# Two cross-attention layers on one core: ScalarE's read of the first V bank moves behind the exps of score tile 3

## The chip, the core and the metric

The kernel runs on one core of a Trainium2 chip. The core has five engines with a queue of instructions each, which run in program order and meet only through semaphores: TensorE (matrix products into the PSUM banks), VectorE, ScalarE (exp and scaled copies), GpSimd and SyncE (here it only starts DMAs). The metric is the device time of one execution in microseconds (us).

## The reference, cut to what matters

Two layers of cross-attention with 20 heads of 32 columns, 8 batches of 100 queries and a context of 722 tokens: 77 text tokens and 645 more tokens ("ip"), which have weights of their own. Each layer takes the softmax over text and over ip apart and adds the two results. Layer 1 also adds a term to the ip scores, computed from the text attention, and multiplies the ip probabilities by a mask.

```python
k, v = heads(text @ Wk), heads(text @ Wv)
k_ip, v_ip = heads(ip @ Wk_ip), heads(ip @ Wv_ip)
text_out = softmax(q @ k.T * scale) @ v
fused = q @ k_ip.T * scale + (0.5 * sem if layer == 1 else 0)   # sem: [b, q, ip token]
ip_out = softmax(fused) * (mask if layer == 1 else 1) @ v_ip
x = (text_out + ip_out) @ Wout + bias + x
```

## The kernel before, in words

The products of context and weights are made from pairs of 16-bit numbers: each operand is split into a high and a low part, and three matmuls (high x high, high x low, low x high) stand for one. So every K or V bank is read twice when it is done: ScalarE writes the high part as a scaled copy (k_unit L1083, v_unit L1091), and VectorE writes the low part as bank minus high part (L1625, L1635). VectorE's instruction waits for ScalarE's (v_high), and its own end sets v_low or k_low, which frees the bank.

A layer has 40 steps u: 8 batches i times 5 groups g of 4 heads. In step u, TensorE does the following in an order written out by hand (window, L808): the V product of step n = u + 1 (five tiles of 24 matmuls, v_tile, three in bank A of `proj`, two in bank B), the six score tiles of step u (score_tile, L695, into the two banks `st`), the weighing of V with the probabilities (weigh, L718), the K product of step k = u + 2 (k_part, in banks A and B again) and the row maxima of the scores of step n (max_scores, L675 and L676). Bank A is therefore used in each step first for V of step n and then for K of step k, and the first k_part of bank A waits for v_low of bank A (L645). Where there is no step k, rows of the output product stand in its place (out_tile).

ScalarE's order in a step (L1133): for each of the six score tiles two exps, one for the high part in 16 bits (L1107) and one in 32 bits (L1108). The end of both is p_high. Score tile j + 2 goes to the same bank and waits for it, and so do the low parts of the probabilities, made by VectorE (tiles 0, 2, 4, L1670) and GpSimd (tiles 1, 3, 5, L1347). Between the tiles stand the reads of the two V banks, in layer 0 slices of the next context (split_context, L1020, groups 1 and 2), and the copy of the transposed output (o_turn, L1114), which frees the buffer `rows` for its next use. In layer 1 VectorE adds the semantic term to each score tile first (add_semantic, L1751), and ScalarE's exps wait for that addition. VectorE's order has its part of the first V bank (L1635) behind prob_low of tile 2 and ahead of add_semantic of tiles 4 and 5.

Some steps of layer 1 hold more (for the first seven batches): group 2 the text logits, group 3 the 48 matmuls of text_ip between weigh 2 and k_part, group 4 turn_semantic (L772), six transposes between v_tile 5 and weigh 1, which write `rows` when o_turn's copy has freed it.

Of the kernel before, what the change touches and what calls it, by code (L numbers as in the profile page):

```python
# [71 lines left out]
def xattn_pair_kernel(nc, ctx_d, text_d, x_d, w_d, wq_d, wo_d, bias_d, mask_d, const_d, sel_d, kd, qd, vd, cd, out_d):  # L72
    with ExitStack() as stack:
# [135 lines left out]
        def need(eng, s, n):  # L209

            if n > 0:
                eng.wait_ge(s, n)
# [17 lines left out]
        def sums(u):  # L230

            return NT * (u - STEPS)

        def low_done(eng, u, j):

            if j < 0:
                u, j = u - 1, j + NT
            if u >= 0:
                mine = [t for t in range(NT) if on_pool(t) == on_pool(j)]
                eng.wait_ge(p_low[on_pool(j)], u * len(mine) + mine.index(j) + 1)  # L240
# [35 lines left out]
        for l in range(LAYERS):  # L276
# [5 lines left out]
            for i in range(B):  # L282
                for g in range(G):
                    u = l * STEPS + i * G + g
# [27 lines left out]
        def placed(n, each):  # L312

            return each * (n // 2 + 1)

        def scales(r):

            return rs[:, r % 2] if r < B else rs1[:, r - B]
# [5 lines left out]
        def scaled(eng, r):  # L324

            eng.wait_ge(row_scale, min(r, B) + 1)
# [9 lines left out]
        def exists(u, l):  # L336

            return u < (l + 1) * STEPS
# [643 lines left out]
        def _(act):  # L982
# [33 lines left out]
            def split_context(r, k):  # L1016

                if k % 2:
                    act.wait_ge(ctx_scaled, r * (KT // 2) + (k // 2 + 1))
                nc.scalar.activation(c_part(r % 2, 0)[:, k, :], ctx_raw[:, k, :], ACT.Copy,  # L1020
                                     scale=1.0 if k % 2 else csb[:, r, 0:1]).then_inc(ctx_high, 1)
# [11 lines left out]
            def q_split(r):  # L1033

                act.wait_ge(q_chain, 5 * (r // B) + 5)
                need(act, qw_out, 16 * r)
                if r > B:
                    row_done(act, "logit", r - B - 1)
                nc.scalar.activation(qhl[:, 0, 0:G * S].rearrange("p (g q) -> p g q", g=G), q_rows(r),
                                     ACT.Copy, scale=qs[:, 4:5]).then_inc(q_hi_ok, 1)  # L1040
# [36 lines left out]
            def k_unit(n, c):  # L1077

                act.wait_ge(k_full, 2 * n + (c + 1))
                if c == 0:  # L1080
                    need(act, kw_out[0], 16 * n)
                a, w = (0, N0) if c == 0 else (N0, N1)
                nc.scalar.activation(khl[:, 0, a:a + w], banks[c][:, 0:w], ACT.Copy, scale=VSC).then_inc(k_high, 1)  # L1083

            def v_unit(n, c):

                act.wait_ge(v_full, 2 * n + (c + 1))
                if c == 0:
                    need(act, pv_tile, NT * (n - 1))
                a, b, src = (2, 2 + VA, bankA) if c == 0 else (2 + VA, NT + 1, bankB)  # L1090
                nc.scalar.activation(vst[:, n % 2, a:b, :, D:2 * D].rearrange("p t h d -> p (t h) d"),  # L1091
                                     src[:, 0:(b - a) * P].rearrange("p (n d) -> p n d", d=D), ACT.Copy,
                                     scale=VSC).then_inc(v_high, 1)

            def exps(u, j):

                r = u // G
                if u >= STEPS:
                    act.wait_ge(s_sum, sums(u) + j + 1)
                else:  # L1100
                    act.wait_ge(s_full, u * NT + (j + 1))
                low_done(act, u, j - 3)
                need(act, pv_tile, (u - 1) * NT + j + 1)
                if j == 0:
                    scaled(act, r)
                scale = scales(r)[:, 4:5] if j == 0 else scales(r)[:, 1:2]
                nc.scalar.activation(p_hi[:, j, 0:Q4], st[:, j % 2, 0:Q4], ACT.Exp, scale=scale)  # L1107
                nc.scalar.activation(prob[:, j % 3, :], st[:, j % 2, 0:Q4], ACT.Exp, scale=scale).then_inc(p_high, 1)  # L1108

            def o_turn(u):  # L1110

                row_filled(act, "oT", u)
                i, g = u // G % B, u % G
                nc.scalar.activation(qo[:, g, i * S:(i + 1) * S], rows[:, 0, 0:S], ACT.Copy).then_inc(row_free, 1)  # L1114

            def logits(i):

                r = B + i
                row_filled(act, "logit", i)
                act.wait_ge(probs, i * 5 + 2)  # L1120
                nc.scalar.activation(pr[:, 0:TEXT], rows[0:S, 0, 0:TEXT], ACT.Exp, bias=sm[:, 1:2],
                                     scale=scales(r)[0:S, 0:1]).then_inc(row_free, 1)

            def turn_semantic(i):

                row_filled(act, "semT", i)
                if i >= 2:
                    act.wait_ge(s_sum, sums((B + i - 1) * G))
                nc.scalar.activation(sem_t[:, i % 2, 1:].rearrange("p n q -> p (n q)"), rows[:, 0, 0:(NT - 1) * S],
                                     ACT.Copy)  # L1130
                nc.scalar.activation(sem_t[:, i % 2, 0], rows[:, 1, 0:S], ACT.Copy).then_inc(row_free, 1)

            def window(l, i, g):  # L1133

                u, r = l * STEPS + i * G + g, l * B + i
                n, k = u + 1, u + 2
                more, more2 = exists(n, l), exists(k, l)
                splits = iter(SLICES[4 * (g - 1):4 * g] if l == 0 and i < B - 1 and g in (1, 2) else ())

                def split():  # L1140
                    for k in splits:
                        split_context(r + 1, k)
                        break

                if u % STEPS and more:
                    k_unit(n, 1)
                exps(u, 0)
                if l == 0 and i < B - 1 and g == 1:
                    act.wait_ge(ctx_chain, 5 * (r + 1) + 5)
                    if r >= 1:  # L1150
                        act.wait_ge(c_out[(r + 1) % 2], placed(r - 1, 32))
                    else:
                        act.wait_ge(w_low, 16)
                split()
                exps(u, 1)
                if l and i < B - 1 and g == 2:
                    logits(i + 1)
                split()
                exps(u, 2)
                if more:  # L1160
                    v_unit(n, 0)
                exps(u, 3)
                if u % STEPS:
                    o_turn(u - 1)
                split()
                if l and i < B - 1 and g == 4:
                    turn_semantic(i + 1)
                exps(u, 4)
                if more:
                    v_unit(n, 1)  # L1170
                exps(u, 5)
                split()
                if g == 1 and i < B - 1:
                    q_split(r + 1)
                if more2:
                    k_unit(k, 0)
# [51 lines left out]
            for i in range(B):  # L1228
                for g in range(G):
                    if i == B - 1 and g == G - 1:  # L1230
                        load_weight(1, 0), load_weight(1, 1)
                    window(0, i, g)
# [36 lines left out]
            for i in range(B):  # L1269
                for g in range(G):  # L1270
                    window(1, i, g)
# [789 lines left out]
```

## Time and profile before

| | us |
|---|---|
| median of 3 runs | 1762.08 (1761.41 to 1764.46) |
| the profiled execution, its own time | 1764.17 |
| its span in the trace | 1762.0 |
| TensorE busy | 1742.4 (99%) |
| VectorE busy | 1197.9 (68%) |
| ScalarE busy | 777.5 (44%) |
| GpSimd busy | 426.0 (24%) |

The granted clock of TensorE was full over the whole span. The score tiles run from 137.9 to 1736.9 us of the span, in two loops, one for each layer; in front of each stand the projections and the splitting of the weights. "PE" is a matmul, "PEld" the load of its weights, which can run beside the matmuls ahead of it. A time in brackets behind a row is what the engine idled before it, with the one it waited for.

### The profile page before, as it was taken

Reading aid. Unit: us, or ns where it says so; the run is one execution under the profiler, and the core shown is the slowest. Engines: PE = TensorE matmul, PEld = TensorE weight load, DVE = VectorE, ACT = ScalarE, POOL = GpSimd, SP = SyncE. Lnnn points to the kernel's source line nnn. Section 1 sums busy time; section 2 is a strip of 40 time slices with the busy share of each in tenths; the row PEclk is TensorE's granted clock in tenths of the full one; section 3 lists DMA queues with packets and bytes.
Section 4 is the critical chain, followed back from the end, with each engine's and each line's share of the span. In section 5 each row is a group of like instructions: output and inputs, shape, how many; then the busy total and the mean of one; then the engine's idle time right before and its main releaser. Section 6 shows DMA issues by size and latency. Waiting matters only on the chain.

```text
span 1762.0 us, 51994 instructions
## 1 busy us (share of the span) xinstructions
PE 1742.4 (99%) x22067; PEld 1413.0 (80%) x22067; DVE 1197.9 (68%) x2905; ACT 777.5 (44%) x1569; POOL 426.0 (24%) x523
## 2 busy tenths in 40 slices
PE   8999999999999999999999999999999999999999
PEld 4778888888888888886577888888888888888885
DVE  6877676767676767554745567767676767676674
ACT  3334555455555555543322344534353435344342
POOL 3034342433333333311100112211121212122111
PEclk9999999999999999999999999999999999999999
DMA  8652535343434343444146232423141323233221
GB/s 324 125 163 105 164 112 156 113 134 113 133 115 131 120 126 123 123 126 179 60 82 177 68 94 81 109 75 101 45 138 45 121 69 109 60 99 92 82 66 47
DMA packets 124015, 198.37 MB, mean 113 GB/s; under 512 B 41752, under 2 KB 110760, under 8 KB 116936
## 3 DMA queue, kind: packets, MB, share of 16 engines
q1 hardware_dynamic: 118600, 168.44, 33.1%
q10 hardware_dynamic: 5184, 26.60, 4.0%
q8 instruction: 175, 2.87, 0.7%
q14 instruction: 56, 0.46, 0.1%
HBM read 133.91 MB, written 60.88 MB: 111 GB/s over the span
## 4 chain that ended last, share of the span: by engine, by line
PE 93%; DVE 3%; DMA 2%; ACT 1%; issue 0%; SPq 0%; POOL 0%; ACTq 0%
PE proj L562 65%; PE proj L522 7%; PE pv L718 6%; PE st L695 5%; PE rows L675 4%; PE rows L562 3%; PE rows L676 2%; DMA arena<-k_dram 1%; DMA k_dram<-arena 1%; DVE wparts L1435 1%; PE rows L763 1%; DMA extra<-x_dram 0%; PE rows L726 0%; PE proj L627 0%; DVE t_hl L1478 0%
## 5 line engine op out<-in xcount | busy, mean ns | idle before, releaser
L562 PE MATMUL proj<-w_hl,cbuf 128*128 128x128 f16 x9600 | 601.0, 219 | 1.2 <-ACT odd_both L1072 1.2
L562 PE MATMUL proj<-cbuf,w_hl 128*128 128x322 f16 (+1 forms) x3840 | 591.5, 300 | 0.3 <-DVE arena L1625 0.3
L562 PEld LDWEIGHTS proj<-w_hl,cbuf 128*128 128x128 f16 x9600 | 548.4, 98 | 3.8 <-ACT odd_both L1072 1.9
L562 PEld LDWEIGHTS proj<-cbuf,w_hl 128*128 128x128 f16 x3840 | 367.7, 97 | 163.5 <-DVE arena L1625 0.6
L1347 POOL TENSOR_TENSOR arena<-arena 128x400 f16<-128x400 f32 x240 | 233.8, 974 | 866.8 <-ACT arena L1108 866.7
L1107 ACT ACTIVATE arena<-st,rs 128x400 f16<-128x400 f32 x480 | 287.3, 598 | 268.3 <-DVE st L1751 158.4
L1083 ACT ACTIVATE arena<-proj 128x323 f16<-128x323 f32 (+1 forms) x160 | 70.7, 442 | 490.2 <-PE proj L562 490.2
L1108 ACT ACTIVATE arena<-st,rs 128x400 f32<-128x400 f32 x480 | 285.7, 595 | 0.0
L1670 DVE TENSOR_TENSOR arena<-arena 128x400 f16<-128x400 f32 x240 | 141.8, 591 | 118.2 <-ACT arena L1108 114.6
L718 PEld LDWEIGHTS pv<-arena 128*128 128x128 f16 x3840 | 175.5, 97 | 25.0 <-issue 4.3
L1751 DVE TENSOR_TENSOR st<-st,sem_t 128x400 f32<-128x400 f32 x240 | 135.3, 579 | 87.1 <-PE st L695 85.3
L718 PE MATMUL pv<-arena 128*128 128x34 f16 (+3 forms) x3840 | 192.4, 189 | 0.0
L1642 DVE TENSOR_REDUCE mx<-rows 100x1 f32<-100x77 f32 x320 | 75.7, 236 | 126.4 <-PE rows L676 126.2
L695 PE MATMUL st<-arena 128*128 128x100 f16 x1920 | 151.5, 207 | 2.2 <-DVE arena L1665 1.4
L1646 DVE CUSTOM_DVE_ANT_0 raw<-rows,raw 100x645 bf16<-100x645 f32 x160 | 131.8, 824 | 0.0
L1650 DVE TENSOR_REDUCE mx<-rows 100x1 f32<-100x645 f32 x160 | 131.1, 819 | 0.0
L675 PE MATMUL rows<-arena 96*128 96x512 f16 x320 | 121.3, 379 | 3.5 <-DMA arena<-k_dram 1.8
L695 PEld LDWEIGHTS st<-arena 128*128 128x128 f16 x1920 | 108.8, 97 | 6.9 <-ACT arena L1108 2.2
L1625 DVE SCALAR_TENSOR_TENSOR arena<-proj,arena 128x323 f16<-128x323 f32 (+1 forms) x160 | 79.0, 494 | 49.2 <-ACT arena L1083 46.4
L676 PE MATMUL rows<-arena 96*128 96x229 f16 x320 | 84.0, 262 | 0.0
L1635 DVE SCALAR_TENSOR_TENSOR arena<-proj,arena 128x384 f16<-128x384 f32 (+1 forms) x160 | 77.3, 483 | 2.0 <-ACT arena L1091 2.0
L1091 ACT ACTIVATE arena<-proj 128x384 f16<-128x384 f32 (+1 forms) x160 | 70.8, 442 | 13.4 <-PE proj L562 13.4
(169 smaller groups left out, 1624.9 us busy)
## 6 DMA issues: line engine op xcount, KB each, us to landing
arena<-k_dram SPq DMA_DIRECT2D x240, 185.2 KB, 3.6
k_dram<-arena SPq DMA_DIRECT2D x160, 161.2 KB, 1.9
raw<-ctx_dram SPq DMA_DIRECT2D x16, 1290.0 KB, 7.7
c_dram<-cbuf SPq DMA_DIRECT2D x16, 1290.0 KB, 6.4
cbuf<-c_dram SPq DMA_DIRECT2D x14, 1290.0 KB, 6.3
cbuf<-w_dram ACTq DMA_DIRECT2D x24, 640.0 KB, 8.0
arena<-q_dram SPq DMA_DIRECT2D x48, 125.0 KB, 2.6
w_hl<-w_dram ACTq DMA_DIRECT2D x8, 640.0 KB, 11.5
```

The lines of the kernel that those rows point to most:

```text
L522: mm = nc.tensor.matmul(bank[:, 0:MT], weight[:, c, k], src[:, k], start=(k == 0), stop=(k == CT - 1))
L562: mm = nc.tensor.matmul(out, x[a](k), w[b](k), start=(k == 0 and m == 0), stop=(k == KT - 1 and m == 2))
L675: nc.tensor.matmul(rows[:, 0, :], q, kp[0:IPO, n % 2, h, 0:512], start=True, stop=True)
L695: mm = nc.tensor.matmul(st[:, j % 2, h * S:(h + 1) * S], kp[:, u % 2, h, a:b], qp[:, r % 2, q_col(g, h):q_col(g, h) + S], start=True, stop ...
L718: mm = nc.tensor.matmul(out, p[:, j, h * S:h * S + P], v, start=(j == 0 and h % 2 == 0 and m == 0), stop=(j == NT - 1 and h % 2 == 1 and m ...
L1107: nc.scalar.activation(p_hi[:, j, 0:Q4], st[:, j % 2, 0:Q4], ACT.Exp, scale=scale)
L1108: nc.scalar.activation(prob[:, j % 3, :], st[:, j % 2, 0:Q4], ACT.Exp, scale=scale).then_inc(p_high, 1)
L1347: nc.gpsimd.tensor_tensor(p_lo[:, j, 0:Q4], prob[:, j % 3, :], p_hi[:, j, 0:Q4], ALU.subtract).then_inc(p_low[1], 1)
L1646: last = nc.vector.tensor_tensor_reduce(out=junk, in0=rows_f[0:S, IPO:KW], in1=semq[r % 2], scale=1.0, scalar=LOWEST, op0=ALU.add, op1=ALU ...
L1650: last = nc.vector.tensor_reduce(mx[:, 1, h:h + 1], rows_f[0:S, IPO:KW], AX.X, ALU.max)
L1670: nc.vector.tensor_tensor(p_lo[:, j, 0:Q4], prob[:, j % 3, :], p_hi[:, j, 0:Q4], ALU.subtract).then_inc(p_low[0], 1)
L1751: nc.vector.tensor_tensor(tile, tile, term, ALU.add).then_inc(s_sum, 1)
```

## The change

In ScalarE's order of each step, the read of the first V bank (v_unit(n, 0)) stands behind the two exps of score tile 3 in place of ahead of them. It concerns the 78 steps that have a next one in their layer. No other engine's order changes.

```diff
@@ -1157,9 +1157,9 @@
                     logits(i + 1)
                 split()
                 exps(u, 2)
+                exps(u, 3)
                 if more:
                     v_unit(n, 0)
-                exps(u, 3)
                 if u % STEPS:
                     o_turn(u - 1)
                 split()
```

ScalarE in an ordinary step of layer 1, before; the first two rows are the exps of tile 2, `proj` is the V bank (the first bank is the one read as 12x32, the second 8x32), `st` a score tile, `rows` the transposed output:

```order
L1107 ACTIVATE arena<-st,rs 128x400 [waits pv_tile,p_low_pool,s_sum]
L1108 ACTIVATE arena<-st,rs 128x400
L1091 ACTIVATE arena<-proj 128x12x32 [waits pv_tile,v_full]
L1107 ACTIVATE arena<-st,rs 128x400 [waits pv_tile,p_low_dve,s_sum]
L1108 ACTIVATE arena<-st,rs 128x400
L1114 ACTIVATE qo<-rows 128x100 [waits row_full]
L1107 ACTIVATE arena<-st,rs 128x400 [waits pv_tile,p_low_pool,s_sum]
```

The same place now:

```order
L1107 ACTIVATE arena<-st,rs 128x400 [waits pv_tile,p_low_pool,s_sum]
L1108 ACTIVATE arena<-st,rs 128x400
L1107 ACTIVATE arena<-st,rs 128x400 [waits pv_tile,p_low_dve,s_sum]
L1108 ACTIVATE arena<-st,rs 128x400
L1091 ACTIVATE arena<-proj 128x12x32 [waits pv_tile,v_full]
L1114 ACTIVATE qo<-rows 128x100 [waits row_full]
L1107 ACTIVATE arena<-st,rs 128x400 [waits pv_tile,p_low_pool,s_sum]
```

The read has gone from the place ahead of the exps of tile 3, which wait for the addition on the tile (s_sum), to the place ahead of the copy of the transposed output.

ScalarE in a step of layer 0 with group 1, before and now; L1020 is a slice of the next context:

```order
L1020 ACTIVATE cbuf<-raw,csb 128x645
L1107 ACTIVATE arena<-st,rs 128x400 [waits pv_tile,p_low_pool,s_full]
L1108 ACTIVATE arena<-st,rs 128x400
L1091 ACTIVATE arena<-proj 128x12x32 [waits pv_tile,v_full]
L1107 ACTIVATE arena<-st,rs 128x400 [waits pv_tile,p_low_dve,s_full]
L1108 ACTIVATE arena<-st,rs 128x400
L1114 ACTIVATE qo<-rows 128x100 [waits row_full]
L1020 ACTIVATE cbuf<-raw 128x645 [waits ctx_scaled]
```

```order
L1020 ACTIVATE cbuf<-raw,csb 128x645
L1107 ACTIVATE arena<-st,rs 128x400 [waits pv_tile,p_low_pool,s_full]
L1108 ACTIVATE arena<-st,rs 128x400
L1107 ACTIVATE arena<-st,rs 128x400 [waits pv_tile,p_low_dve,s_full]
L1108 ACTIVATE arena<-st,rs 128x400
L1091 ACTIVATE arena<-proj 128x12x32 [waits pv_tile,v_full]
L1114 ACTIVATE qo<-rows 128x100 [waits row_full]
L1020 ACTIVATE cbuf<-raw 128x645 [waits ctx_scaled]
```

Here the exps wait for the score tile itself (s_full), and the read passes the same two rows.

## Rows read from the trace of the kernel before

**Rows 1.** The page's chain of work that ended last: share of the span by engine.
```profile
PE 93%; DVE 3%; DMA 2%; ACT 1%; issue 0%; SPq 0%; POOL 0%; ACTq 0%
```

**Rows 2.** Two stretches: length, busy us of each engine, clock, DMA share, GB/s.
```profile
150.00:800.00 650.00, 646.84 (x9271) 547.75 (x9267) 454.47 (x1082) 335.38 (x692) 223.37 (x248) 1.00 0.40 125
...
1000.00:1700.00 700.00, 697.99 (x9681) 586.08 (x9679) 488.83 (x1315) 305.79 (x649) 138.16 (x190) 1.00 0.31 89
```

**Rows 3.** Timeline, ordinary step of layer 1: start us, us, engine, line, operation.
```profile
1200.90 0.34 PE L695 MATMUL st<-arena 128*128 128x100 f16 x4
...
1201.28 0.58 DVE L1751 TENSOR_TENSOR st<-st,sem_t 128x400 f32<-128x400 f32 x1 [0.93 <-PE st L695]
...
1201.35 0.49 ACT L1091 ACTIVATE arena<-proj 128x384 f16<-128x384 f32 x1
...
1201.90 0.59 ACT L1107 ACTIVATE arena<-st,rs 128x400 f16<-128x400 f32 x1
...
1202.25 0.55 DVE L1635 SCALAR_TENSOR_TENSOR arena<-proj,arena 128x384 f16<-128x384 f32 x1
...
1202.87 0.25 ACT L1114 ACTIVATE qo<-rows 128x100 f32<-128x100 f32 x1
...
1203.48 1.06 DVE L1751 TENSOR_TENSOR st<-st,sem_t 128x400 f32<-128x400 f32 x2 [0.68 <-PE st L695]
...
1203.66 0.67 PEld L562 LDWEIGHTS proj<-cbuf,w_hl 128*128 128x128 f16 x6
...
1203.68 0.99 PE L562 MATMUL proj<-cbuf,w_hl 128*128 128x323 f16 x6
```

**Rows 4.** Timeline, first V bank of layer 1, both readers waiting.
```profile
980.31 0.49 ACT L1091 ACTIVATE arena<-proj 128x384 f16<-128x384 f32 x1 [2.21 <-PE proj L562]
...
980.83 0.56 DVE L1635 SCALAR_TENSOR_TENSOR arena<-proj,arena 128x384 f16<-128x384 f32 x1 [0.88 <-ACT arena L1091]
```

**Rows 5.** Timeline, ordinary step of layer 0.
```profile
459.89 0.34 PE L695 MATMUL st<-arena 128*128 128x100 f16 x4
...
460.27 0.59 ACT L1107 ACTIVATE arena<-st,rs 128x400 f16<-128x400 f32 x1
...
461.24 0.25 ACT L1114 ACTIVATE qo<-rows 128x100 f32<-128x100 f32 x1
...
462.64 0.67 PEld L562 LDWEIGHTS proj<-cbuf,w_hl 128*128 128x128 f16 x6
```

**Rows 6.** Timeline, a step of layer 0 with group 1.
```profile
425.68 0.50 ACT L1091 ACTIVATE arena<-proj 128x384 f16<-128x384 f32 x1
...
426.05 0.61 ACT L1107 ACTIVATE arena<-st,rs 128x400 f16<-128x400 f32 x1
...
426.53 0.62 ACT L1108 ACTIVATE arena<-st,rs 128x400 f32<-128x400 f32 x1
...
427.20 0.20 PEld L695 LDWEIGHTS st<-arena 128*128 128x128 f16 x4 [0.19 <-ACT arena L1108]
...
427.60 1.09 PEld L562 LDWEIGHTS proj<-cbuf,w_hl 128*128 128x128 f16 x9
```

**Rows 7.** Timeline, a step of layer 1 with group 4.
```profile
1261.86 0.49 ACT L1091 ACTIVATE arena<-proj 128x384 f16<-128x384 f32 x1
...
1263.74 0.46 PEld L772 LDWEIGHTS rows<-const,raw 100*128 100x128 f32 x5 [0.37 <-issue]
...
1265.09 0.67 PEld L562 LDWEIGHTS proj<-cbuf,w_hl 128*128 128x128 f16 x6
```

**Rows 8.** Who waited for whom: us in total, times, longest us.
```profile
PEld rows L683 <- DVE mxh L1658: 15.4, 77, 0.8
...
PE rows L772 <- ACT qo L1114: 1.6, 7, 0.2
...
PE rows L683 <- DVE mxh L1658: 0.6, 1, 0.6
```

## The prediction, made before the changed kernel had run

> **What bounds the kernel now.** I read the page's chain first, then the stretches of the two layers, the waits of TensorE and of its weight loads, and at last single steps of the timeline. In the chain the reader is to see that TensorE holds 93% of the time [rows 1]. In the long loop of layer 0 it leaves 650.00 - 646.84 = 3.2 us open, in that of layer 1 700.00 - 697.99 = 2.0 us [rows 2]. So the most that any reordering of ScalarE can win in both loops is 5.2 us, 0.3% of the time, while each new wait of TensorE lands on the end in full. The question is what TensorE next asks of bank A of the product `proj`: k_part of the step after next overwrites it and waits for v_low, which VectorE sets when it has read the bank, and VectorE subtracts what ScalarE wrote, so it waits for ScalarE's read.
>
> **The change.** It removes and adds no instruction. In each of the 78 steps that have a next one in their layer ScalarE's read of the first V bank goes behind the two exps of score tile 3. On ScalarE it passes only those two; ScalarE's DMAs stand outside the steps and keep their places. Queued behind the read in its new place: the copy of the transposed output (L1114), a context slice, the exps of tile 4. Queued behind VectorE's part of that bank (L1635): in layer 1 the additions for tiles 4 and 5, in layer 0 a context slice or row maxima.
>
> Do the exps start sooner? In an ordinary step of layer 1 the read runs 1201.35 to 1201.84; the addition on tile 3 ends 1201.28 + 0.58 = 1201.86, and the exps start at 1201.90 [rows 3]. They wait for that addition, 0.04 behind it, and the read lay wholly inside this wait. In an ordinary step of layer 0 score tile 3 ends 459.89 + 0.34 = 460.23 and the exps start at 460.27 [rows 5]. So in both the exps of tile 3 can't start sooner, ScalarE loses a free place for its read, and the read is pushed behind 0.97 us of exps (1201.90 to L1114's start at 1202.87 [rows 3]).
>
> Layer 1, ordinary step [rows 3]: read of V at 1202.87, end + 0.49 = 1203.36. VectorE takes over 0.03 behind such an end: 980.31 + 0.49 = 980.80, start 980.83 [rows 4]. So L1635 runs 1203.39 to 1203.94 (0.55 each). TensorE follows a VectorE or ScalarE end 0.05 later (426.53 + 0.62 = 427.15, load at 427.20 [rows 6]), so its first weight load of k_part is possible at 1203.99 and now stands at 1203.66 [rows 3]: a wait of 0.33, say 0.34 us. Before, L1635 ended at 1202.80 and there were 0.86 us to spare. All links of the chain hang on TensorE's own score tile 3, so a later start in the step before does not pay any of it back: each step pays.
>
> How many steps? Groups 0, 1 and 2 of eight batches, 24. In group 3 of the first seven, the 48 long matmuls of text_ip stand ahead of k_part, in group 4 the turn of the semantic term pushes k_part to 1265.09 - 1261.86 = 3.23 us behind the old read, against 2.31 in the ordinary step [rows 7, 3]; both cover 0.34. In the last batch group 3 has no k_part. 24 x 0.34 = **8.2 us**.
>
> Group 4 of the first seven batches pays elsewhere. The copy L1114 now stands behind the moved read: it starts one spacing of that read later, 426.05 - 425.68 = 0.37 us [rows 6]. TensorE's turn of the semantic term waits for this copy today (0.37 us idle ahead of its weight load [rows 7], 1.6 us of matmul time in seven cases [rows 8]). 7 x 0.37 = **2.6 us**. In the other groups the next user of that row buffer comes behind weigh 2, when the copy (new end 1203.24 + 0.25 = 1203.49) is done.
>
> VectorE's additions for tiles 4 and 5 follow L1635: 1203.48 becomes about 1203.86, so the exps of tile 4 and the second V read come 0.38 us later. What waits for these are weigh 4 and k_part on bank B, several matmul groups behind; I cost it at nothing, and if that cover were gone it would be 0.38 per step more.
>
> Layer 0, ordinary step [rows 5]: read 461.24 to 461.73, L1635 461.76 to 462.31, load possible at 462.36, wanted at 462.64: 0.28 us to spare, no wait. In groups 0 and 4 VectorE has context maxima in front of L1635 anyway.
>
> Layer 0, group 1 of seven batches: here ScalarE lags, since it splits the context, and the exps of tile 3 really start sooner, at 425.68 where the read stood, in place of 426.05. The wait of 0.19 us in front of score tile 5 goes [rows 6], 7 x 0.19 = 1.3 us and no more. But bank A: read 426.64 (two spacings of 0.48 behind 425.68), end 427.14, L1635 427.17 to 427.72, load possible at 427.77, today 427.60. What comes late next is this: the gained 0.19 turns into a wait in front of k_part and 0.17 beyond it. 7 x 0.17 = **1.2 us**.
>
> Sum: 8.2 + 2.6 + 1.2 = 12.0 us. Against the profiled execution (1764.2 us, span 1762.0) that is 1776.2; it stood 2.1 us above the median of the runs, 1762.1, and on this median I forecast **1774.1 us**.
>
> Bounds. From below: TensorE's loads run ahead of its matmuls, so a load that waits is not always a matmul that waits. The transpose of the maxima shows it: 77 waits of its load are 15.4 us, but its matmul is listed with 0.6 us, once [rows 8]. There the matmul in front is a long one. In front of k_part stand the short ones of weigh 2, and load and matmul of k_part begin 0.02 apart (1203.66 and 1203.68 [rows 3]), so I take the load's wait as the matmul's. Would each wait be softened by 0.15, the sum is 24 x 0.19 + 7 x 0.22 + 7 x 0.02 = 6.2 us. The Trainium skill ("TensorE: Matmul & The Clock Gate", on what happens when a matmul is issued) says that the queue pulls weight loads ahead of running matmuls while the matmuls keep their order; by that rule the softening is there wherever a long matmul runs in front, and for the transpose the trace agrees (15.4 us of loads, 0.6 us of matmuls).
> From above: if the exps and the read did not overlap at their ends (0.59 + 0.59 in place of 0.97), every chain is 0.21 longer: 24 x 0.55 + 7 x 0.37 + 7 x 0.38 = 18.5 us.
> The Trainium skill ("ScalarE: Activation LUTs", What ACT_TABLE_LOAD costs) gives an activation 186 ns plus 0.833 per element, 93 more for a scale by pointer and 93 less back to back. As an estimate that spaces the exps by 0.52 us, where the trace has 0.49; by the page the sum would be some 2 us larger, and the trace decides.
>
> **Rivals.**
> *Half price*: the softening above. For it: the transpose [rows 8]. Against: the 0.02 between load and matmul. +6 us, 1768.
> *Covered*: VectorE's read fits, because the moved read finds a gap or k_part starts later than I read. For it: in layer 0 the spare place exists. Against: every ordinary step of layer 1 repeats those times [rows 3]. Only the seven copies remain, 2.6 us, 1764.7, or nothing.
> *Knock-on*: the 0.38 us on the exps of tiles 4 and 5 reaches weigh 4, or layer 0's 0.28 us is used up by slower reads. 24 x 0.38 = 9 us more, 1783. Against: weigh 4 stands two groups of k_part matmuls behind.
> *Faster*: score tile 5 and GpSimd's low part of tile 3 wait for the exps of tile 3, so these set the step wherever ScalarE lags, and the read can wait. It is decided by whether ScalarE is late at tile 3: only the seven steps of layer 0 show that. It would win at most 7 x 0.19 plus one longer first wait, some 1.7 us, 1760.4, and beyond the 5.2 us of open time nothing. It needs that bank A is never late, against [rows 3, 6].
>
> **How the numbers follow.** Full price (1770 to 1778) 0.74; half price 0.10; knock-on or the upper bound 0.07; covered 0.06; faster 0.03. A measurement of this kernel can tell 0.2%, 3.5 us, from no change. Half price and all above it are slower: 0.91. Covered gives within 0.2%; faster, as worked out, stays mostly within it too, and I leave 0.02 for more. The range leaves out the knock-on and the covered case: 1768 to 1779.
>
> **What would show it.** Right: the read of V about 1.5 us later in an ordinary step; in layer 1 a wait of proj's loads for L1635 on the list, about 24 to 31 times and 8 to 10 us; L772 waiting for L1114 with some 0.6 us each; exps of tile 3 as far behind score tile 3 as before; the steps of layer 0 outside group 1 as long as before. Wrong: no such wait in layer 1; ordinary steps of layer 0 longer; a wait of weigh 4 for L1670, or exps of tile 3 that start sooner in layer 1.

## The result: 14.1 us slower, 8 of them in 24 steps of layer 1

The changed kernel takes 1775.87 us (median of 6 runs, 1775.27 to 1777.75), the kernel before 1761.74 us (6 runs, 1761.09 to 1764.46): 14.1 us more, ratio 1.0079 [1.0066, 1.0092]. The forecast was 1774.1 us in a range of 1768 to 1779.

The profiled execution took 1775.68 us (span 1773.5). The page's chain, shares of the span by engine:

```profile
PE 86%; DVE 5%; ACT 4%; issue 2%; POOL 1%; DMA 1%; SPq 0%; ACTq 0%
```

TensorE had 93% of the chain [rows 1]; VectorE and ScalarE now have 9% in place of 4%. The stretches of both layers, columns as in [rows 2]:

```profile
150.00:800.00 650.00, 646.91 (x9266) 547.04 (x9263) 455.35 (x1080) 335.41 (x693) 225.91 (x248) 1.00 0.40 125
1000.00:1700.00 700.00, 691.77 (x9529) 578.54 (x9528) 481.98 (x1295) 301.21 (x641) 136.19 (x187) 1.00 0.31 88
```

In layer 1 TensorE's open time grew from 2.0 to 700.00 - 691.77 = 8.2 us. In layer 0 it did not grow (3.1 us), and yet some of its steps got longer, as shown below: the stretch of before holds 1.6 us in which matmuls waited for K loads, that of the changed kernel none, and this hides the new waits. The waits that answer to [rows 8], and the new ones:

```profile
PEld rows L683 <- DVE mxh L1658: 15.0, 77, 0.8
PEld proj L562 <- DVE arena L1635: 9.3, 31, 0.4
PE proj L562 <- DVE arena L1635: 6.0, 31, 0.3
...
PEld rows L772 <- issue: 5.2, 7, 0.7
...
PE rows L772 <- ACT qo L1114: 4.2, 7, 0.6
...
PEld pv L718 <- POOL arena L1347: 2.7, 7, 0.4
...
PE rows L683 <- DVE mxh L1658: 0.6, 1, 0.6
```

The first two new ones were forecast: k_part waits 31 times for VectorE's part of bank A, and L772 waits longer for the copy L1114. The wait of the weighing (L718) for GpSimd's low part was not. The step that answers to [rows 3], timeline:

```profile
1205.22 0.58 DVE L1751 TENSOR_TENSOR st<-st,sem_t 128x400 f32<-128x400 f32 x1 [0.94 <-PE st L695]
...
1205.83 0.59 ACT L1107 ACTIVATE arena<-st,rs 128x400 f16<-128x400 f32 x1 [0.44 <-DVE st L1751]
...
1206.80 0.49 ACT L1091 ACTIVATE arena<-proj 128x384 f16<-128x384 f32 x1
...
1207.17 0.26 ACT L1114 ACTIVATE qo<-rows 128x100 f32<-128x100 f32 x1
...
1207.32 0.56 DVE L1635 SCALAR_TENSOR_TENSOR arena<-proj,arena 128x384 f16<-128x384 f32 x1 [1.05 <-ACT arena L1091]
...
1207.80 1.05 DVE L1751 TENSOR_TENSOR st<-st,sem_t 128x400 f32<-128x400 f32 x2
1207.93 0.66 PEld L562 LDWEIGHTS proj<-cbuf,w_hl 128*128 128x128 f16 x6 [0.28 <-DVE arena L1635]
1207.94 1.00 PE L562 MATMUL proj<-cbuf,w_hl 128*128 128x323 f16 x6 [0.17 <-DVE arena L1635]
```

The exps of tile 3 start 1205.83 - (1205.22 + 0.58) = 0.03 us behind the addition, as before: nothing was won. ScalarE now idles 0.44 us ahead of them, where it had read V. The read comes 0.97 behind the start of the exps, VectorE's part 0.52 behind the read, k_part's load 0.61 behind that.

To see what a wait costs, the steps are measured: from TensorE's transpose of the maxima (L683), which ends each step, to the next one, less the same step of the kernel before. In us per step, changed kernel:

| layer | groups | steps | longer by |
|---|---|---|---|
| 0 | 0, 3, 4, the last batch | the others | 0 |
| 0 | 1, first seven batches | 7 | -0.02 to 0 |
| 0 | 2, first seven batches | 7 | 0.41 |
| 1 | 0, 1, 2 | 24 | 0.33 to 0.35 (22 of them) |
| 1 | 3, first seven batches | 7 | 0 |
| 1 | 4 | 7 | 0.38 |
| 1 | 3 of the last batch, the last step with a next one | 1 | 0.30 |

24 x 0.34 + 7 x 0.38 + 7 x 0.41 + 0.30 = 14.0 us. The other steps are within 0.03, except single ones, mostly those in which, in one of the two executions, TensorE waits for a DMA of K (1.8 us of such matmul waits in the profiled execution of before, none listed in the changed kernel's; the first step of layer 1's batch 3 is 0.05 shorter here and 1.2 longer in e11). Such waits come and go from kernel to kernel, and by them the spans of the two profiled executions differ by only 11.5 us. So costs are read here from repeated steps, and the medians only with their intervals.

### The profile page after: what moved, and what is told of

The parts are those of the page before. It is cut to its first block, busy times and chain, and to the rows that moved or that the text cites. A ratio compares the mean times of both kernels' runs of the same rounds, so it can differ in the third digit from the quotient of the medians.

```text
span 1773.5 us, 51994 instructions
## 1 busy us (share of the span) xinstructions
PE 1745.6 (98%) x22067; PEld 1413.2 (80%) x22067; DVE 1199.7 (68%) x2905; ACT 776.7 (44%) x1569; POOL 428.3 (24%) x523
## 4 chain that ended last, share of the span: by engine, by line
PE 86%; DVE 5%; ACT 4%; issue 2%; POOL 1%; DMA 1%; SPq 0%; ACTq 0%
PE proj L562 61%; PE proj L522 6%; PE pv L718 5%; PE rows L675 4%; PE st L695 4%; PE rows L562 3%; ACT arena L1108 2%; PE rows L676 2%; DVE arena L1635 1%; DMA mask<-mask_dram 1%; DVE st L1751 1%; ACT arena L1091 1%; POOL arena L1347 1%; DVE wparts L1435 1%; PE rows L763 1%
## 5 line engine op out<-in xcount | busy, mean ns | idle before, releaser
L1347 POOL TENSOR_TENSOR arena<-arena 128x400 f16<-128x400 f32 x240 | 234.0, 975 | 875.0 <-ACT arena L1108 874.9
L1670 DVE TENSOR_TENSOR arena<-arena 128x400 f16<-128x400 f32 x240 | 145.7, 607 | 97.8 <-ACT arena L1108 94.6
L718 PEld LDWEIGHTS pv<-arena 128*128 128x128 f16 x3840 | 174.8, 97 | 27.1 <-issue 4.3
L718 PE MATMUL pv<-arena 128*128 128x34 f16 (+3 forms) x3840 | 192.5, 189 | 0.3
L1650 DVE TENSOR_REDUCE mx<-rows 100x1 f32<-100x645 f32 x160 | 131.0, 818 | 0.0
L675 PE MATMUL rows<-arena 96*128 96x512 f16 x320 | 121.3, 379 | 1.5 <-DVE mx L1650 0.5
L1635 DVE SCALAR_TENSOR_TENSOR arena<-proj,arena 128x384 f16<-128x384 f32 (+1 forms) x160 | 77.8, 486 | 60.8 <-ACT arena L1091 60.8
```

The source lines that it names most:

```text
L675: nc.tensor.matmul(rows[:, 0, :], q, kp[0:IPO, n % 2, h, 0:512], start=True, stop=True)
L718: mm = nc.tensor.matmul(out, p[:, j, h * S:h * S + P], v, start=(j == 0 and h % 2 == 0 and m == 0), stop=(j == NT - 1 and h % 2 == 1 and m ...
L1347: nc.gpsimd.tensor_tensor(p_lo[:, j, 0:Q4], prob[:, j % 3, :], p_hi[:, j, 0:Q4], ALU.subtract).then_inc(p_low[1], 1)
L1650: last = nc.vector.tensor_reduce(mx[:, 1, h:h + 1], rows_f[0:S, IPO:KW], AX.X, ALU.max)
L1670: nc.vector.tensor_tensor(p_lo[:, j, 0:Q4], prob[:, j % 3, :], p_hi[:, j, 0:Q4], ALU.subtract).then_inc(p_low[0], 1)
```

## Experiments

The first four runs compare parts of the change, against a kernel before of 1764.22 us. Each `late` is the condition under which the read stands in its new place.

**e1, the change in layer 0 alone**, and **e2, in layer 1 alone**:

```diff
                 exps(u, 2)
-                if more:
+                late = l == 0        # e2: l == 1
+                if more and not late:
                     v_unit(n, 0)
                 exps(u, 3)
+                if more and late:
+                    v_unit(n, 0)
```

> The read of the first V bank behind the exps of tile 3 in layer 0 alone; layer 1 as before. Theory A (the cost of layer 0 sits in group 2 of the first seven batches, where GpSimd's context slice and the low part of tile 3 queued behind it come late): +0.41 us in each of those seven steps, nothing in the other groups, +2.9 us in all. Theory B (my prediction: a wait for bank A in group 1): seven times 0.17, +1.2 us. Theory C (the difference between the two traces in layer 0 is only chance in the waits for k_dram loads): within 1 us, and no step longer by a fixed amount.

> The read behind the exps of tile 3 in layer 1 alone. Theory A (TensorE waits for bank A 24 times by 0.34 us, for the copy L1114 seven times by 0.37, and once by 0.3 in front of the output product of the last step): +11.1 us, the layer 1 steps exactly as long as with the whole change, so that both layers add up to the whole. Rival (the two layers act on each other over the weights and the turn between them): less or more than the rest that layer 0 leaves of 14.1 us.

e1: 1767.84 us against 1764.22, ratio 1.0015 [1.0004, 1.0025]. Steps: group 2 +0.40 to 0.41, seven times, group 1 nothing, layer 1 nothing. e2: 1774.13, ratio 1.0053 [1.0036, 1.0071]; layer 0 nothing, layer 1 as in the changed kernel (0.34, 0.38 and 0.34 for the last). The steps of the two halves add up to those of the whole, so neither cost depends on the other layer's change.

**e3, layer 1 alone, and in group 4 the copy ahead of the moved read:**

```diff
+                if late and g == 4 and u % STEPS:
+                    o_turn(u - 1)
                 if more and late:
                     v_unit(n, 0)
-                if u % STEPS:
+                if u % STEPS and not (late and g == 4):
                     o_turn(u - 1)
```

> As the change in layer 1 alone, but in group 4 the copy of the transposed output (L1114) stands ahead of the moved read. Theory A: the seven group 4 steps lose nothing any more (0.37 less each, 2.6 us less than the change in layer 1 alone), since k_part has over 0.5 us to spare there for a read 0.25 us later; +8.5 us. Rival (group 4 is long because the exps of tiles 4 and 5 are late): those steps stay 0.37 longer, +11.1 us.

Group 4's steps fall from +0.38 to 0 (within 0.01), the ordinary ones stay at 0.34. The waits of L772:

```profile
PEld rows L772 <- issue: 2.6, 7, 0.4
PE rows L772 <- ACT qo L1114: 1.6, 7, 0.2
```

So group 4 pays for the copy and for nothing else. The time itself was not lower than e2's: 1776.14 us, ratio 1.0058 [1.0035, 1.0081], 6.2 to 14.3 us. In the profiled execution the stretch between the two loops, in which the projections of layer 1 stand and which the edit doesn't touch, is 4.2 us longer. The interval holds the 8.5 us of the steps, and e2's time too: only the steps tell e3 from e2.

**e4, only where the steps say it is free** (layer 0 without group 2 of the first seven batches, and layer 1, group 3 of the same):

```diff
+                late = (l == 0 and (g != 2 or i == B - 1)) or (l == 1 and g == 3 and i < B - 1)
```

> The change only in steps where it should cost nothing: layer 0 except group 2 of the first seven batches, layer 1 only group 3 of the first seven. 32 + 7 = 39 steps have the new order. Theory A: no step differs by more than 0.03 us, time within 0.5 us of before. Prediction's theory B for group 1: +1.2 us. Rival (the new order costs a little everywhere, as ScalarE idles ahead of the exps and then works longer): 39 steps x 0.1 or more, +4 us.

1765.03 us against 1764.22, ratio 1.0003 [0.9993, 1.0013]. The steps with group 1 are within 0.02 although their k_part waits (2.6 us of its loads in seven cases). Nothing is gained in them either.

The next four runs ask what a wait of k_part costs, and what happens in group 2. The time of the kernel before is 1762.07 us beside them.

**e6, the read behind the copy too**, in all steps:

```diff
                 exps(u, 3)
-                if more:
-                    v_unit(n, 0)
                 if u % STEPS:
                     o_turn(u - 1)
+                if more:
+                    v_unit(n, 0)
```

> The dose: the read behind the exps of tile 3 and behind the copy L1114 (0.25 us more, by the spacing of L1114 to what follows). Theory A (the chain score tile 3, addition, exps, read, VectorE's part, k_part sets the step in layer 1): 24 ordinary steps wait 0.34 + 0.21 to 0.25 = 0.55 to 0.59, group 4 waits nothing for the copy, layer 0 ordinary steps have 0.28 to spare and lose 0 to 0.03, group 1 and 2 lose up to 0.25 and 0.4: 13.7 + 0.5 + 2.9 to 4.6 = +17 to +19 us. Rival (the additions of tiles 4 and 5 are what is late): the same order of VectorE, so about the same; it differs in the next run.

1779.21 us, ratio 1.0093 [1.0076, 1.0110]. Ordinary steps of layer 1 +0.48 to 0.49, group 4 nothing, group 2 of layer 0 +0.54 to 0.55, group 1 +0.04 to 0.06. The read ends 0.15 later than in the changed kernel, where 0.21 to 0.25 was expected, since it begins while the copy still runs. The step is 0.15 longer: 0.15 of lateness buys 0.15 of length, with no softening.

**e7, the first two maxima matmuls ahead of the first k_part**, layer 1, groups 0 to 2, on the changed kernel:

```diff
+                first = l == 1 and g < 3
+                if first:
+                    max_scores(n, 0)
                 if more2:
                     k_part(k, 0, 0, begun)
-                max_scores(n, 0)
+                if not first:
+                    max_scores(n, 0)
```

> The whole change, and TensorE does the first row maxima of the next step (2 matmuls, 0.32 us by their spacing) ahead of the first k_part in groups 0, 1, 2 of layer 1, where they stood behind six of its matmuls. Theory A: TensorE has work while bank A is read, the 24 waits of 0.34 fall to 0.02, 7.7 us less than the whole change, so +6.4 us. Rival (the layer 1 cost comes from the additions for tiles 4 and 5 and the exps behind them, which stay as late as in the whole change): +14.1 us, no less. If the maxima have a wait of their own so early (k_dram loads, the row buffer), some of it comes back under another name.

The ordinary steps fall from +0.34 to +0.02 or 0.03: with other work in front of k_part, the lateness of bank A costs next to nothing. VectorE's additions for tiles 4 and 5 still come late here, so these cost nothing either. Its loads are still listed with a long wait, its matmuls no longer outside layer 0 (there 1.8 us, as in the changed kernel):

```profile
PEld proj L562 <- DVE arena L1639: 7.9, 30, 0.5
...
PE proj L562 <- DVE arena L1639: 1.8, 7, 0.3
```

(L1639 is L1635 with four lines more in front.) The time: 1772.37 us, ratio 1.0056 [1.0041, 1.0071], 7.2 to 12.5 us above before. The steps give 24 x 0.02 + 0.1 + 2.7 + 2.9 + 0.3 = 6.5. The rest of the run's difference stays open; the profiled execution has 1.8 us of K waits, as the one of before has.

**e8, the read between the two exps of tile 3**, all steps of the kernel before:

```diff
-                if more:
-                    v_unit(n, 0)
-                exps(u, 3)
+                exps(u, 3, (lambda: v_unit(n, 0)) if more else None)   # called behind the first exp
```

> The read between the two exps of tile 3 in every step. Theory A: the read ends 0.48 us sooner than in the change, so bank A is free at 1203.51 on the clock of the ordinary step of before, ahead of the 1203.66 at which k_part wants it: no wait there. p_high of tile 3 comes 0.37 late: score tile 5 may wait 0.1 in each of the 31 steps that have no other cover. The copy L1114 is 0.37 late as before: group 4 loses 0.37 seven times, group 2 of layer 0 its 0.41. 2.6 + 2.9 + 0 to 3 = +5.5 to +8.5 us. Rival (what costs is every later end of ScalarE's work on tile 3, whichever piece is last): as the whole change, +14 us.

1770.69 us, ratio 1.0047 [1.0032, 1.0062]. No wait of k_part for L1635 is listed any more, and group 2 of layer 0 is at +0.02. Yet 30 of the 32 steps of groups 0 to 3 of layer 1 are 0.14 to 0.15 longer (the other two are the first and that of batch 3), and VectorE's maxima start 0.15 later in them. The second exp of tile 3 now ends 0.38 later, and score tile 5 needs its bank. TensorE's row of score tiles 4 and 5 in an ordinary step, first before, then e8:

```profile
1203.11 0.51 PE L695 MATMUL st<-arena 128*128 128x100 f16 x8
```

```profile
1204.04 0.66 PE L695 MATMUL st<-arena 128*128 128x100 f16 x8
```

The row is 0.15 longer, the whole cost of the step. The wait falls inside a group of matmuls that the view shows as one row, so no wait is listed. In the changed kernel, where the exps keep their time, that row is 0.51 as before. So for the read there is no free place behind the exps' first half either. The time, 8.6 us above before, lies at the end of the 5.5 to 8.5 that was expected, with two errors in it: group 2 costs nothing in place of 2.9, and score tile 5 costs 32 x 0.145 = 4.6 in place of 0 to 3.

**e5, group 2: GpSimd's low part of tile 3 ahead of its context slice**, on the changed kernel:

```diff
-                    chores = iter((lambda: split_context(r + 1, 5), lambda: split_context(r + 1, 7)))
+                    chores = iter((lambda: None, lambda: split_context(r + 1, 5), lambda: split_context(r + 1, 7)))
```

> The whole change, and in group 2 of layer 0 GpSimd makes the low part of tile 3 (and of tile 5) before its context slice in place of behind it. Theory A (weigh 3 waits for GpSimd's low part, which stands behind the slice that waits for ScalarE's late copy of it): the seven group 2 steps lose their 0.41 us again, 2.9 us less than the whole change, so +11.2 us against before. Rival (weigh 3 is late because VectorE and GpSimd hold each other up over their common reads, whatever the order): at least half of the 0.41 stays.

1776.89 us, ratio 1.0082 [1.0067, 1.0097]; the steps of group 2 stay at +0.41. The wait for GpSimd is gone from the list, and another stands there:

```profile
PEld rows L675 <- DVE mx L1650: 3.3, 8, 0.8
PE rows L675 <- DVE mx L1650: 2.4, 8, 0.7
```

The theory that GpSimd's queue order sets the cost fell. The timelines of such a step tell more. Before:

```profile
444.13 0.88 DVE L1500 SCALAR_TENSOR_TENSOR cbuf<-raw,csb,cbuf 128x645 f16<-128x645 f32 x1
...
445.10 1.41 POOL L1323 TENSOR_TENSOR cbuf<-raw,cbuf 128x645 f16<-128x645 f32 x1 [2.53 <-ACT cbuf L1020]
...
446.30 0.64 DVE L1670 TENSOR_TENSOR arena<-arena 128x400 f16<-128x400 f32 x1 [1.29 <-ACT arena L1108]
...
447.34 0.81 DVE L1650 TENSOR_REDUCE mx<-rows 100x1 f32<-100x645 f32 x1
```

The changed kernel, the same step:

```profile
443.56 0.49 ACT L1091 ACTIVATE arena<-proj 128x384 f16<-128x384 f32 x1
...
444.09 0.56 DVE L1635 SCALAR_TENSOR_TENSOR arena<-proj,arena 128x384 f16<-128x384 f32 x1 [0.73 <-ACT arena L1091]
...
444.56 0.88 DVE L1500 SCALAR_TENSOR_TENSOR cbuf<-raw,csb,cbuf 128x645 f16<-128x645 f32 x1
...
444.90 1.81 POOL L1323 TENSOR_TENSOR cbuf<-raw,cbuf 128x645 f16<-128x645 f32 x1 [2.72 <-ACT cbuf L1020]
...
445.91 1.24 DVE L1670 TENSOR_TENSOR arena<-arena 128x400 f16<-128x400 f32 x1 [0.46 <-ACT arena L1108]
446.68 1.28 POOL L1347 TENSOR_TENSOR arena<-arena 128x400 f16<-128x400 f32 x1
...
447.55 0.81 DVE L1650 TENSOR_REDUCE mx<-rows 100x1 f32<-100x645 f32 x1
...
448.00 0.28 PEld L718 LDWEIGHTS pv<-arena 128*128 128x128 f16 x8 [0.39 <-POOL arena L1347]
```

Before, VectorE's context slice L1500 was over at 445.01, when GpSimd's slice L1323 began. Now VectorE waits 0.73 us for the moved read, its slice begins behind that and runs to 445.44, and GpSimd's slice, which begins at 444.90, lasts 1.81 in place of 1.41 us. VectorE's low part L1670 then lasts 1.24 in place of 0.64, and VectorE's maxima (L1650) and GpSimd's low part L1347 are both late, by 0.6 us measured from the exps of tile 2. (Of the 0.6 us, 0.18 is a later start of GpSimd's slice, which waits for ScalarE, and 0.40 its longer run.) e5 has the same 1.80 and 1.24: it took away only one of the two that wait. Over the whole stretch from 150 to 800 us the groups of these lines show it too (count, then busy us and mean ns), before:

```profile
L1670 DVE TENSOR_TENSOR arena<-arena 128x400 f16<-128x400 f32 x111 | 68.3, 615 | 104.2 <-ACT arena L1108 100.8
L1323 POOL TENSOR_TENSOR cbuf<-raw,cbuf 128x645 f16<-128x645 f32 x28 | 39.2, 1409 | 21.0 <-ACT cbuf L1020 21.0
```

The changed kernel:

```profile
L1670 DVE TENSOR_TENSOR arena<-arena 128x400 f16<-128x400 f32 x111 | 72.4, 653 | 85.1 <-ACT arena L1108 82.1
L1323 POOL TENSOR_TENSOR cbuf<-raw,cbuf 128x645 f16<-128x645 f32 x28 | 41.9, 1509 | 19.1 <-ACT cbuf L1020 19.1
```

The same instructions take 4.1 and 2.7 us more: 0.6 and 0.4 in each of seven steps.
It is always the instruction that starts second that gets longer: VectorE's slice, over whose end GpSimd's begins, takes 0.88 us in both kernels, and GpSimd's slice of before takes 1.41 with L1670 over its end. The Trainium skill ("SBUF — State Buffer", Who interferes with whom) says that VectorE and GpSimd share a port pair as an exclusive lock, and its summary that of a VectorE instruction with two SBUF inputs and a GpSimd instruction that reads SBUF the second one is blocked until the first is done. The trace agrees, less a constant: when GpSimd's slice starts, VectorE's has 0.54 us to go, and it is 0.40 longer; when L1670 starts, GpSimd's slice has 0.80 to go, and it is 0.67 longer than alone (0.57). The durations count the hold as busy time.

**e10, VectorE's slice ahead of its part of V**, group 2 of layer 0, on the changed kernel:

```diff
+                if l == 0 and g == 2:
+                    low()
                 if more:
                     v_unit(n, 0)
                 add_semantic(u, 4)
```

> The change, and in layer 0, group 2, VectorE's second context slice (L1500) ahead of its part of the first V bank (L1635), where VectorE idles 0.73 us in the changed kernel. Collision theory: the late read of V pushes that slice over the start of GpSimd's slice (L1323), which then runs 1.81 in place of 1.41 us, VectorE's low part L1670 runs 1.24 in place of 0.64, and everything behind is late by the 0.4 us per step. With the slice out of the way GpSimd's takes 1.41 again, L1670 0.6 to 0.7, and the seven steps of group 2 are as long as before the change: 14.1 - 2.9 = 11.2 us slower than before. Rival, lateness of VectorE's own order behind the moved read: L1635 ends 0.14 later still, and the steps stay 0.41 or more longer, 14.1 us or more.

1773.33 us against 1762.62, ratio 1.0066 [1.0053, 1.0078]. The seven steps are as long as before the change (within 0.03), everything else is as in the changed kernel. The timeline:

```profile
441.65 0.88 DVE L1500 SCALAR_TENSOR_TENSOR cbuf<-raw,csb,cbuf 128x645 f16<-128x645 f32 x1
...
442.46 0.56 DVE L1635 SCALAR_TENSOR_TENSOR arena<-proj,arena 128x384 f16<-128x384 f32 x1
...
443.28 1.41 POOL L1323 TENSOR_TENSOR cbuf<-raw,cbuf 128x645 f16<-128x645 f32 x1 [2.72 <-ACT cbuf L1020]
...
444.28 0.84 DVE L1670 TENSOR_TENSOR arena<-arena 128x400 f16<-128x400 f32 x1 [1.26 <-ACT arena L1108]
```

L1323 is back to 1.41 us, L1670 to 0.84 (0.64 before, so not the whole of it), and the read of V and the start of GpSimd's slice are as late as in the changed kernel. So the collision was the cost, not the late read itself. That the hold is a shared port is what the Trainium skill says; the runs show that the slice that starts beside the other is slow, and one behind the other is not.

**e11, the change with all three costs covered** (the edits of e7, of e10 and the order of e3 in group 4; e7's edit moves two matmuls, not four):

> The change with all of its three costs covered: in layer 0, group 2, the context slice ahead of VectorE's part of V; in layer 1, group 4, the copy (L1114) ahead of the moved read; in layer 1, groups 0 to 2, the four maxima matmuls of head 0 ahead of the first k_part. If these three are all that the move costs, only 24 x 0.02 + 0.11 + 0.3 (last step) = 0.9 us is left over before, ratio 1.0005. If a cost is only passed on to a later wait: 0.34 in the ordinary steps or 0.41 in group 2 remains, 3 us or more.

1764.91 us, ratio 1.0011 [1.0002, 1.0020], 0.4 to 3.5 us. The steps sum to 24 x 0.02 + 0.1 + 0.3 = 0.9 us. The interval holds them. So the four places account for the change, and the read in its new place brings nothing even when nearly all of its costs are gone.

**e9, the kernel before with the copy ahead of the exps of tile 3**, layer 1, group 4:

```diff
                 if more:
                     v_unit(n, 0)
+                ahead = l == 1 and g == 4
+                if ahead and u % STEPS:
+                    o_turn(u - 1)
                 exps(u, 3)
-                if u % STEPS:
+                if u % STEPS and not ahead:
                     o_turn(u - 1)
```

> The kernel before, with the read of V in its old place, and in layer 1, group 4, the copy of the transposed output (L1114) ahead of the exps of tile 3, into ScalarE's wait for the addition on that tile. The waits of TensorE's L772 for that copy go (0.37 us of its load, 0.2 us of its matmul, seven cases): the seven steps are 0.2 us shorter, 1.4 us in all, ratio 0.9992, below what the runs can tell and visible only in the steps. Rival: the copy delays the exps of tile 3, or the gain is lost in the weighing behind: nothing.

1759.75 us (1758.75 to 1761.40, 11 runs) against 1762.62 (21 runs), ratio 0.9983 [0.9974, 0.9992]: this order is 1.4 to 4.6 us faster than the kernel before. The timeline of such a step, which answers to [rows 7]:

```profile
1260.69 0.26 ACT L1114 ACTIVATE qo<-rows 128x100 f32<-128x100 f32 x1
...
1260.86 0.59 ACT L1107 ACTIVATE arena<-st,rs 128x400 f16<-128x400 f32 x1
...
1261.79 0.46 PEld L772 LDWEIGHTS rows<-const,raw 100*128 100x128 f32 x5
1261.84 0.60 PE L772 MATMUL rows<-const,raw 100*128 100x100 f32 x5
```

L772 no longer waits. Each of the seven steps is 0.40 to 0.41 shorter, 2.8 us, twice what was expected: the wait had been priced by its matmul (1.6 us for seven), and the step gives back a little more than what the load waited (0.37 [rows 7]).

## Why the prediction was right, and where it was not

The direction, the main mechanism and the total were right. Two terms of the sum were wrong, 1.2 us too much and 2.9 too little, and a third of 0.3 was missing. They partly offset each other, which is luck, though the forecast would have been in its range without it: with group 2's 2.9 us alone added it is 1777.0.

- *ScalarE gains nothing by starting tile 3's exps first.* Right: 0.03 us behind the addition, as before.
- *Layer 1, ordinary steps: 24 x 0.34 = 8.2 us.* Right in place, count and size (0.33 to 0.35 in 22 of the 24 steps; the first has 0.44, and one is that of batch 3 in which a K load differs). The chain of hand-offs was read from rows to 0.01 us: exps 0.97, read 0.52, VectorE 0.61, then the load.
- *Group 3 free.* Right, 0.
- *Layer 1, group 4: 7 x 0.37 = 2.6 us by the copy L1114.* Right, and e3 shows it is this copy.
- *Layer 0, group 1: 7 x 0.17 = 1.2 us.* Wrong: 0. The wait of k_part is there, and its size is right: its first matmul comes 0.19 us later in the step, where 0.17 was forecast. Timeline:

```profile
427.38 0.64 ACT L1107 ACTIVATE arena<-st,rs 128x400 f16<-128x400 f32 x1
427.40 0.67 PEld L562 LDWEIGHTS proj<-cbuf,w_hl 128*128 128x128 f16 x6 [0.34 <-DVE arena L1635]
427.41 0.86 PE L562 MATMUL proj<-cbuf,w_hl 128*128 128x323 f16 x5 [0.24 <-DVE arena L1635]
```

  But these steps are set by something behind it. VectorE's first maxima (L1650) start 11.34 us behind the L683 ahead of the step in both kernels (418.56 to 429.90 before, 418.17 to 429.51 after) and free the row buffer of TensorE's next maxima (L675). TensorE's first maxima of the step are 0.19 later than before (10.49 in place of 10.30 behind that L683), its next ones only 0.06 (12.28 in place of 12.22). VectorE's last maxima are still 0.04 late, and the instruction behind them (L1656), which leads to the transpose that ends the step, takes up the rest. It is held by GpSimd's scaling of the context, before and in the changed kernel:

```profile
433.86 2.48 POOL L1317 TENSOR_TENSOR raw<-raw,csb 128x645 f32<-128x645 f32 x2
435.66 0.71 DVE L1656 TENSOR_SCALAR mxh<-mx 100x8 f16<-100x8 f32 x1
```

```profile
433.47 2.48 POOL L1317 TENSOR_TENSOR raw<-raw,csb 128x645 f32<-128x645 f32 x2
435.31 0.67 DVE L1656 TENSOR_SCALAR mxh<-mx 100x8 f16<-100x8 f32 x1
```

  L1656 takes 0.18 us in the other groups and 0.65 to 0.72 here, and in all seven of these steps of both kernels it ends 0.03 to 0.04 behind GpSimd's second scaling. So GpSimd sets the end of these steps; this is read from the traces, and no run moved that scaling. The prediction looked at whether k_part would be late and not at what the step was waiting for behind it.
- *Layer 0, ordinary steps free, group 2 among them.* Right for groups 0, 3 and 4, wrong for group 2: 7 x 0.41 = 2.9 us, and this is the largest miss. The prediction treated group 2 as ordinary because its k_part has 0.28 us to spare, and it has. What the prediction left out is that VectorE's context slice, queued behind its part of V, moves over GpSimd's slice. It named that slice as queued behind and did not say who waits for it or who works beside it. Longer steps of layer 0 outside group 1 stood among its own signs of being wrong, and these seven are such steps.
- *The last batch adds nothing beyond its groups 0 to 2.* Off by 0.30 us, once: where there is no step k the output product takes bank A and waits in the same way.
- *Exps of tiles 4 and 5 later, at no price.* Right in layer 1: e6 and e7 show steps that follow the first wait alone.
- *Bound from below, half price.* Refuted by e6 and by the steps (the 0.15 by which it softens each wait came from no row): the full 0.34, k_part's first matmul 9.05 us behind its L683 in place of 8.72. Matmuls of k_part are listed with only 6.0 / 31 = 0.19 us and its loads with 9.3 / 31 = 0.30, less than the step loses, since the profile lists idle time from the end of what ran before, not from when the instruction would have started.
- *Bound from above.* The exps and the read overlap at their ends as in [rows 3], and the 0.21 was not paid.
- *Covered, knock-on, faster.* None of them happened. In e4 even the steps where ScalarE lags, and where the wait of score tile 5 goes from the list, win nothing.

By terms the forecast was 12.0 us and the steps give 14.0: -1.2 (group 1) + 2.9 (group 2) + 0.3 (last step).

## What to carry to other kernels

Find the waits of an engine in order and use them as places: a read that fits into a wait is free there, and behind it it costs what its chain is late, wherever the one that waits for it has no other work to do first (0.34 us in 24 steps, nothing in group 3, 0.02 in e7). The copy that TensorE waited for was worth 2.8 us in the same place. Price a late operand by when TensorE would have started, step against step; the waits that are listed were 0.19 to 0.30 for a cost of 0.34, and the one of e4, listed at 2.6 us, cost nothing where the step was set further on. When an instruction is pushed back, look at each one queued behind it on its engine for what it now runs beside on another engine, not only for who waits for it.

## What of the hardware was not expected

Where one of the instructions below starts on VectorE or GpSimd while one on the other of the two engines runs, the first keeps its time, and the second is longer by what the first has left at that moment, less some 0.14 us:

| second, behind first | first has left | second longer by |
|---|---|---|
| GpSimd's slice L1323 behind VectorE's L1500, changed kernel | 0.54 | 0.40 (1.81 in place of 1.41) |
| VectorE's low part L1670 behind L1323, changed kernel | 0.80 | 0.67 (1.24 in place of 0.57) |
| the same, before | 0.21 | 0.07 |
| the same, e10 | 0.41 | 0.27 |
| VectorE's small L1656 behind GpSimd's L1317, before | 0.68 | 0.53 (0.71 in place of 0.18) |

The same holds for all 48 pairs of L1500, L1670, L1323 and L1347, in either trace, in which the first had more than 0.2 us left: the constant lies between 0.13 and 0.20.

The hold is counted as busy time, so the waits don't show it; the mean duration of a line, compared between two kernels or between steps that have the neighbour and steps that don't, does.
